# Eight PSUM outputs per hand-over instead of two, in the step-size and B/C stage of a Mamba and ternary-FFN layer

## The reference

```python
xn = _layernorm(x)
x, z = in_proj(xn)                       # each [4096, L]
x = silu(causal_conv4(x) + conv_b)
x_dbl = einsum('bdl,kd->blk', x, x_proj_w)             # 160 rows
dt_lo, Bmat, Cmat = x_dbl[..., :128], x_dbl[..., 128:144], x_dbl[..., 144:]
delta = softplus(einsum('blr,dr->bld', dt_lo, dt_proj_w) + dt_proj_b)
h_t = h_{t-1} * exp(delta_t * A) + delta_t * B_t * x_t     # [4096, 16]
y_t = sum_n(h_t * C_t)
out = out_proj((y + x * D) * silu(z))
```

## Time and profile before

| what | value |
|---|---|
| time, median of 2 runs | 13189.26 us (13183.64 and 13194.88) |
| profiled execution, its own time | 13361.88 us |
| span of its slowest core (core 1) | 13360.3 us |
| spans of its 8 cores | 13100.0 to 13360.3 us |
| busy on core 1: PE, DVE, ACT, POOL | 5419.6, 7269.9, 4323.7, 766.3 us |
| DMA, mean over the span | 101 GB/s |

### The profile page before, as it was taken

The page is one execution under the profiler, slowest core; times in us unless marked ns, Lnnn a source line. Parts: engine busy times, 40 slices in busy tenths (PEclk is TensorE's granted clock), DMA queues, the critical chain, the costliest instruction groups (busy, mean ns, idle before and its releaser), DMA issues.

```text
span 13360.3 us, 105861 instructions; the slowest of 8 cores (13100.0 to 13360.3 us)
## 1 busy us (share of the span) xinstructions
PE 5419.6 (41%) x28160; PEld 3127.3 (23%) x28160; DVE 7269.9 (54%) x8002; ACT 4323.7 (32%) x7239; POOL 766.3 (6%) x1286
## 2 busy tenths in 40 slices
PE   0116666433323323323323323323323336756666
PEld 0002222122212212212212212212212222322222
DVE  6661111268768868858858858868858830000011
ACT  1222222144344444434434434434434421001000
POOL 0002222100000000000000000000000000000000
PEclk9998888766666656656656656656656666776777
DMA  2106666612212212212212212212212233243354
GB/s 84 33 22 194 196 193 185 163 53 91 94 43 89 83 59 90 85 57 90 87 54 91 86 54 88 88 55 89 90 58 82 88 137 135 101 154 129 135 188 161
DMA packets 607805, 1354.38 MB, mean 101 GB/s; under 512 B 43504, under 2 KB 387696, under 8 KB 533232
## 3 DMA queue, kind: packets, MB, share of 16 engines
q1 hardware_dynamic: 539632, 1154.60, 26.3%
q0 software_dynamic: 67584, 193.02, 4.0%
HBM read 1154.51 MB, written 192.94 MB: 101 GB/s over the span
## 4 chain that ended last, share of the span: by engine, by line
DVE 44%; DMA 18%; PE 14%; issue 11%; ACT 11%; SPq 1%; DVEq 1%; ACTq 0%; POOL 0%; POOLq 0%
DVE PA L688 13%; DVE PA L692 9%; PE pb L790 8%; ACT dA L676 5%; DMA wgusp<-PA 5%; DVE PA L669 4%; PE pb L858 4%; DMA PA<-wuT 3%; DMA PA<-psp 3%; DVE PA L693 2%; DVE PA L300 2%; DMA PA<-ygsp 2%; DVE PA L588 2%; DVE PA L592 2%; DMA PA<-wgT 2%
## 5 line engine op out<-in xcount | busy, mean ns | idle before, releaser
L503 PE MATMUL pb<-PA 128*128 128x256 bf16 x8192 | 1414.3, 347 | 4372.7 <-DVE PA L529 4357.5
L688 DVE TENSOR_TENSOR_SCAN PA<-dA,hcar,PA 128x256 f32<-128x256 f32 x3840 | 2494.5, 726 | 39.3 <-ACT dA L676 14.6
L676 ACT ACTIVATE dA<-PA,a_sb 128x256 f32<-128x256 bf16 x3840 | 1961.5, 511 | 476.9 <-DVE PA L669 134.7
L503 PEld LDWEIGHTS pb<-PA 128*128 128x128 bf16 x8192 | 980.0, 122 | 4727.5 <-issue 4441.3
L873 DVE TENSOR_TENSOR PA<-pb,PA 128x512 f32<-128x512 f32 x64 | 44.3, 692 | 2418.8 <-PE pb L858 2418.8
L790 PE MATMUL pb<-PA 128*128 128x512 bf16 x4096 | 1060.8, 431 | 630.7 <-DMA PA<-psp 630.7
L414 PE MATMUL pb<-PA 128*128 128x512 bf16 x4096 | 983.0, 405 | 545.7 <-DVE PA L398 384.7
L676 ACT ACT_TABLE_LOAD x240 | 307.9, 1283 | 2699.1 <-DVE PA L669 2699.1
L507 PE MATMUL pb<-PA 128*128 128x256 bf16 x8192 | 1160.5, 303 | 0.0
L692 DVE TENSOR_TENSOR PA<-PA 128x4096 bf16<-128x4096 f32 x256 | 1132.9, 4425 | 27.7 <-DVE PA L688 1.4
L507 PEld LDWEIGHTS pb<-PA 128*128 128x128 bf16 x8192 | 902.5, 110 | 201.9
(11 more groups left out here) (101 smaller groups left out, 5420.3 us busy)
## 6 DMA issues: line engine op xcount, KB each, us to landing
PA<-wgusp SPq DMA_DIRECT2D x512, 1024.0 KB, 4.8
PA<-winT SPq DMA_DIRECT2D x32, 2048.0 KB, 21.0
PA<-wgT SPq DMA_DIRECT2D x256, 256.0 KB, 4.8
wgusp<-PA POOLq DMA_DIRECT2D x512, 128.0 KB, 4.3
PA<-wuT SPq DMA_DIRECT2D x256, 256.0 KB, 4.5
PA<-wdT SPq DMA_DIRECT2D x64, 1024.0 KB, 6.3
PA<-ygsp SPq DMA_DIRECT2D x16, 4096.0 KB, 13.6
PA<-xrow SPq DMA_DIRECT2D x32, 1024.0 KB, 4.9
```

The lines of the kernel that those rows point to most:

```text
L503: I("tensor", lambda e, k=k, bank=bank, sl=sl: e.matmul(bank[:, 0:TCH], wgu_sl[sl][:, 0, k, :], qwin[:, k, :], start=(k == 0), stop=(k == ...
L676: exp_sc[n] = I("scalar", lambda e, dt=dt, n=n: e.activation(dAs_t[n][:], delta[:, dt, :], AF.Exp, scale=a_sb[:, dt, n:n + 1]), "sc")
L688: I("vector", lambda e, n=n, dt=dt: e.tensor_tensor_scan(hall[:, n, :], dAs_t[n][:], dbx_b[:, n, :], hcar[:, dt, n:n + 1], ALU.mult, ALU.a ...
```

## The change

The two loops become one loop over 8 waves of 8 outputs (`w`, `s`; output number `j = 8w + s`, the first 32 for the step size, the others for B and C). Eight slots, two in each of the banks 4 to 7, take a wave's outputs. TensorE waits once for the last eviction of the wave before and issues eight matmuls; ACT waits once for the last of them and issues its eight evictions. Matmuls, evictions, their shapes and their order are as before; lines from L631 on have new numbers (L634 and L639 for the matmuls, L646 and L653 for the evictions, L660 to L663 and L665 for the softplus).

```diff
--- before.py
+++ after.py
@@ -622,32 +622,36 @@
             I("scalar", lambda e: e.activation(dtlo[:], p_xd, AF.Copy), "sc")
             sc_xp = I("scalar", lambda e: e.activation(bc_sb[:], p_bc, AF.Copy), "sc")
 
-            ev_dt_sc = [0, 0]
-            W("tensor", "sc", sc_xp)
-            for dt in range(KDI):
-                half = dt % 2
-                bank = [pb[5], pb[7]][half][:, 0:TCH]
-                W("tensor", "sc", ev_dt_sc[half])
-                te_dt = I("tensor", lambda e, dt=dt, bank=bank: e.matmul(
-                    bank, wdt_bf[:, dt * 128:(dt + 1) * 128], dtlo[:],
-                    start=True, stop=True), "te")
-                W("scalar", "te", te_dt)
-                ev_dt_sc[half] = I("scalar", lambda e, dt=dt, bank=bank: e.activation(
-                    delta[:, dt, :], bank, AF.Identity, bias=dtb_sb[:, dt:dt + 1]), "sc")
-
-            ev_bc_sc = [0, 0]
-            for n in range(32):
-                half = n % 2
-                bank = [pb[6], pb[4]][half][:, 0:TCH]
-                W("tensor", "sc", ev_bc_sc[half])
-                te_bc = I("tensor", lambda e, n=n, bank=bank: e.matmul(
-                    bank, oneh[:, n * 128:(n + 1) * 128], bc_sb[:],
-                    start=True, stop=True), "te")
-                W("scalar", "te", te_bc)
-                dst = b_all if n < 16 else c_all
-                dn = n if n < 16 else n - 16
-                ev_bc_sc[half] = I("scalar", lambda e, dst=dst, dn=dn, bank=bank: e.activation(
-                    dst[:, dn, :], bank, AF.Copy), "sc")
+            wave_sc = sc_xp
+            slots = [pb[4 + s // 2][:, (s % 2) * TCH:(s % 2 + 1) * TCH]
+                     for s in range(8)]
+            for w in range(8):
+                W("tensor", "sc", wave_sc)
+                te_w = 0
+                for s in range(8):
+                    j = w * 8 + s
+                    if j < KDI:
+                        te_w = I("tensor", lambda e, j=j, s=s: e.matmul(
+                            slots[s], wdt_bf[:, j * 128:(j + 1) * 128], dtlo[:],
+                            start=True, stop=True), "te")
+                    else:
+                        n = j - KDI
+                        te_w = I("tensor", lambda e, n=n, s=s: e.matmul(
+                            slots[s], oneh[:, n * 128:(n + 1) * 128], bc_sb[:],
+                            start=True, stop=True), "te")
+                W("scalar", "te", te_w)
+                for s in range(8):
+                    j = w * 8 + s
+                    if j < KDI:
+                        wave_sc = I("scalar", lambda e, j=j, s=s: e.activation(
+                            delta[:, j, :], slots[s], AF.Identity,
+                            bias=dtb_sb[:, j:j + 1]), "sc")
+                    else:
+                        n = j - KDI
+                        dst = b_all if n < 16 else c_all
+                        dn = n if n < 16 else n - 16
+                        wave_sc = I("scalar", lambda e, dst=dst, dn=dn, s=s: e.activation(
+                            dst[:, dn, :], slots[s], AF.Copy), "sc")
 
             ve_sp_add = 0
             for hh in range(4):
```

## The result

| | before | changed |
|---|---|---|
| median | 13234.84 us (10 runs, 13170.52 to 13435.16) | 13371.02 us (12 runs, 13287.85 to 13479.53) |
| ratio | 1 | 1.0107, 95% interval 1.0061 to 1.0152 |
| span of the profiled execution, slowest core | 13360.3 us | 13290.8 us |

A forecast was written before the change was run, and what follows sets the result against it. ACT's row of evictions with its waits was taken as the path; per chunk 32.65 + 1.34 + 15.05 = 49.04 us against 35.71, 107 us over 8 chunks, added to 13189.3: 13296 us, range 13225 to 13370.

The forecast's parts named there:

- What bounds the stage: Projection evictions at each chunk's head: ACT's row of 64 with its waits is the path, moving DVE one for one.
- The stage after: Same stage with serial waves: matmuls and evictions never overlap, 49.04 us per chunk against 35.71, 107 us in all.
- The clock: TensorE in the stage: first wave at the higher clock level, waves 2 to 8 at the lower, bubbles 2.15 us each.
- What else moves: Shared banks and unit matmuls starting some 10 us later, behind the stage: costed at nothing, the delay hidden.
- Against which time: Whole kernel: the 107 us carried over onto the unprofiled median of 13189.3 us, giving 13296 us.
- C: Dense stages after the scan: a better granted clock there outweighs the loss, not slower, 13061 us; chance 0.06.
- A: TensorE's bursts in the stage: all stay at the higher clock level, +61 us, 13250 us; chance 0.12.
- B: TensorE's bursts in the stage: weight loads don't overlap, +177 us, 13366 us; chance 0.08.
- D: The stage's waves: they overlap after all, stage 2.5 us less per chunk, 13169 us; chance 0.01.

The follow-up runs named there:

- e8: B and C evicted by ACT two outputs at a time, against e1, whose groups of 4 it keeps: 13099.5 us, one run.
- e1: Groups of 4 outputs with TensorE one group ahead, against the changed kernel's serial waves of 8: 13212.3 us, ratio 1.0023 to the kernel before.
- e2: Sixteen serial waves of 4 outputs, against the changed kernel's eight of 8: 13342.4 us, one run.
- e6: Sixty-four serial waves of 1 output, against the changed kernel's eight of 8: 13427.9 us, ratio 1.0208 to the kernel before.
- e3_filled: The changed kernel with 16 of the unit matmuls issued behind each wave's 8: 13257.7 us, one run.
- e10_again2: The changed kernel timed a third time, without an edit: 13281.7 us, ratio 1.0094 to the kernel before.
- e4_dve_bc: The kernel before with B and C evicted by DVE in pairs, TensorE alternating step-size and B/C matmuls: 13103.1 us, ratio 0.9916.
- e7_split22: The kernel before with ACT evicting only 22 step-size outputs, in pairs, DVE the last 10 and B and C: 12995.5 us, ratio 0.9877.

## Why the prediction was right or wrong

**What bounds the stage: right.** The path was ACT's row with its waits. In the four experiments that left all evictions to ACT and added nothing on TensorE (e8, e1, e2, e6), DVE's waits were 599, 633, 776 and 918 us, each within 2 us of what was expected, and the scan moved with them.

**The stage after: right, to 1%.** 49.35 us were measured in the second chunk against 49.04 (0.28 of the difference is one gap between two evictions of 0.37 instead of 0.09 us); evictions in 4.44 and 3.72 us (4.47 and 3.69), pauses of 1.33 and 2.15 (1.34 and 2.15), bursts of 1.03 and 1.87 (1.04 and 1.86). The mean of DVE's waits over the cores rose from 644.2 to 751.1, by 106.9 us; the sum said 107. The price of a burst came from the earlier trace rows, another line's matmuls of the same shape and level, and it held. The lower estimate that rested on the Trainium skill ("TensorE: Matmul & The Clock Gate", section "Back-to-back issue gap"), 0.10 us for each further matmul and +56 us, did not: a further one cost (1.03 - 0.27) / 7 = 0.11 us in the first wave and (1.86 - 0.37) / 7 = 0.21 in the others.

**The clock: right.** Waves two to eight stood at the lower level (0.50 in the window above), and the first at the upper one. e3_filled shows that this choice was worth up to 0.83 us per wave. The reason that I gave, how small a part of a wave TensorE works, is not shown: with TensorE given more to do between the bursts, the level was still down in several waves.

**What else moves: nearly right.** Costed at nothing, it was 8 us in the first pair of profiles: DVE's waits at L529 rose from 762.9 to 767.6 us on average and its waits for the loads of xsp at L583 from 148.5 to 152.1. With the 107 they make the scan's 116. e10_again2 has 763.5 and 148.1, so these few microseconds are not the change's.

**Against which time: wrong, and this is the step that failed.** "I carry over the 107 us as they are: 13296 us" put an exact difference on the median of two runs, 13189.3, and against C I wrote that "both runs of before agree within 0.1%". Ten runs of the same kernel have a median of 13234.8 and go from 13170.5 to 13435.2. Of the 75 us between forecast and result, 46 are this, and 29 are the difference itself (136 less 107), of which the scan explains at most 9. That the time fell 1 us outside the range and not inside it is chance: later the changed kernel's medians were 13317.6 and 13281.7 us, with 13168.9 and 13153.2 for before beside them. The profiled execution had the warning in it: its own time of 13361.9 and cores 235 us apart. I used them for a rival and not for the range. Where the time varies is plain from the first profile of before: dense stages of 2302 to 2315 us on cores 2 to 5 and of 2485 to 2517 on the others, while the scan was 8126 to 8144 on all of them. As the metric is the slowest of eight cores, it takes the worst of these each time. A stretch of 40 us of the down projection in which TensorE never pauses shows what differs (before, cores 1 and 2):

```profile
11520.00:11560.00 40.00, 40.00 (x151) 16.41 (x150) 0.00 (x0) 1.20 (x2) 1.08 (x2) 0.80 0.04 14
...
11520.00:11560.00 40.00, 40.00 (x187) 18.09 (x186) 0.00 (x0) 1.79 (x3) 1.08 (x2) 1.00 0.04 14
```

Core 1 has a mean granted clock of 0.80 and gets through 151 matmuls, core 2 has 1.00 and gets through 187. The slow pace, a matmul every 0.26 us, holds in this execution for cores 0, 1, 6 and 7 over most of the down projection, in e1_ahead4's for cores 2, 3, 6 and 7, and in the profiled execution of the changed kernel for none. What decides it is open. A range of 107 us plus and minus a fraction was right for the difference; for the time it had to add some 100 us upwards.

**Rivals.** A (clock up, +61) and B (no overlap of weight loads, +177) are excluded by the timeline. C exists as scatter, in both directions; nothing shows it as an effect of the change. D is excluded by the eight groups.

## What to carry to other kernels

Fewer hand-overs are no gain in themselves: count what the consumer waits for. When one engine produces and one consumes, a producer one group ahead hides its whole time, however many hand-overs there are, as long as its burst and two hand-overs are shorter than the consumer's work on a group (1.30 against 1.89 us for B and C in e1_ahead4; before, with single outputs, they were not, and ACT idled 0.18 us for every two). A serial wave pays two hand-overs and the whole burst; e1_ahead4 and e2_wave4 have the same groups of four and differ in that, by 17.7 us per chunk. Where a third engine idles beside such a row, giving it part of the row gained more (170 us in the scan) than any order of waiting could. And before a time is forecast, look at how far the cores of one execution lie apart and in which stages: what a change does in its own stage can be known to a microsecond while the time is not known to a hundred.

## What the runs showed of the hardware

- Matmuls of 256 columns that alternate between weights on 128 and on 32 rows start 0.32 us apart at the lower level (e4_dve_bc), against 0.213 for rows of one kind. In pairs of one kind (e7_split22) two of each take 1.13 us instead of 1.29. The cause wasn't tested.
- The same burst of eight took 1.03 or 1.86 us within one stage of one execution, as the granted clock changed between waves (e3_filled). Keeping TensorE at work between the bursts raised it in some waves only.
- Dense stages that no edit touches differ by up to 9% between the cores of one execution (2302 to 2517 us), while the scan differs by 0.2% (8126 to 8144 us). In the slower ones TensorE's 128x512 matmuls follow each other every 0.26 instead of every 0.22 us, at a granted clock of 0.80 instead of 1.00 (before, cores 1 and 2).
